# Fewer matmuls for a short contraction tile: three products of 82 rows packed into two tiles by copies within SBUF

## The chip, the cores and the metric

The kernel runs on one core of a Trainium2 chip. The metric is device time in microseconds (us) of one execution. Engines are called PE (TensorE, matmuls), ACT (ScalarE), DVE (VectorE), POOL (GpSimd) and SP (the engine that issues the DMAs).

## What is computed

A cross-attention with a gate, for 8 batches of 100 rows of width 1024 and contexts of 722 rows of width 512, in float32:

```
memory_proj = einsum('bme,de->bmd', memory, W_mem)
scores = einsum('bnd,bmd->bnm', hidden, memory_proj) / sqrt(1024)
attn = softmax(scores)
memory_context = einsum('bnm,bmd->bnd', attn, memory_proj)
gate = sigmoid(einsum('bnf,df->bnd', concat(hidden, memory_context), W_gate) + b_gate)
out = rmsnorm(hidden + gate * memory_context, norm_w)
```

The kernel multiplies by W_mem after the attention: it forms q = hidden x W_mem (width 512), scores = q x context, pc = probabilities x context (100 x 512 for a batch), and applies W_mem to pc at the end.

## The kernel before

Every float32 operand of a product is split into two fp32r tiles, a rounded `hi` (an ACT copy) and a rest `lo` = value - hi (a DVE subtraction, function `minus`, line 711). A product is then three matmuls: hi x hi, hi x lo, lo x hi.

The program is one stream of instructions for each engine, written out by hand in the order in which they run; semaphores tie the streams together. It has four stages: q for all rows; eight attention steps (`step(b, ...)`, one for each batch, in the PE, ACT and DVE streams); W_mem applied to the result (`mc_block`); the gate and the norm.

One attention step on PE:

- scores: 24 matmuls of 362 columns (line 384);
- `fill(1)`: 24 matmuls of the gate product with hidden (line 290), which need nothing of this step and lie beside the softmax;
- six transposes of the probabilities (line 398) into PSUM, once ACT's exponential is done;
- `fill(2)`: 18 more gate matmuls, beside the splitting of the transposed probabilities into `pt_hi` and `pt_lo`;
- pc: the contraction over the 722 context rows. 722 = 5 x 128 + 82, so there are MT = 5 full tiles and one of ML = 82 rows, each with three matmuls of 512 columns: 18 (line 408);
- `fill(3)`: 6 gate matmuls, while ACT scales pc;
- four transposes of pc (line 415).

The context rows (tensor `ctxN`) are loaded into `cn_stage` in three DMAs: tiles 0 to 2 (line 217), tiles 3 and 4 (line 221), and the 82 end rows (line 223). ACT rounds them into `cn_hi` (`split_ctx`, lines 542, 545 and 546) and DVE makes `cn_lo`, in two parts: part 0 (tiles 0 to 2) late in the step before, part 1 (tiles 3, 4 and the end) in the step itself. `ct_stage`, `ct_hi` and `ct_lo` are the same for the transposed context, which the scores use. All loads are issued by SP on one queue, in a fixed order: in `ahead(b)` one weight tile for the step after next (line 204), two loads of `ctxT` (line 210), then `load_ctx(b + 1)`. Each waits for the split that frees its stage buffer. In the ACT stream a step is: exponential (line 593), rounding of a weight tile (523), part 1 of the context, `pt_hi` from PSUM (600, 602), the transposed context (534), scaling pc (607), saving gate and pc (588, 612), part 0 of the next context. In the DVE stream: two maxima (780), their combination (782), the weight tile's lo part, the reciprocal of the row sums (786), `pt_lo`, part 1 of the context, the transposed context, then the saving of a gate tile (774) and q_lo.

The three matmuls of the 82-row tile are these, the last of the accumulation:

```
for lhs, rhs, part in ((pt_hi, cn_hi, 0), (pt_hi, cn_lo, 1), (pt_lo, cn_hi, 2)):
    done = nc.tensor.matmul(bank(PCB, C, N), lhs[0:rows, t, :], rhs[0:rows, t, :],
                            start=t == 0 and part == 0, stop=t == MT and part == 2)
```

Of the kernel before, what the change touches and what calls it, by code (L numbers as in the profile page):

```python
# [42 lines left out]
def build(nc, xT, ctxT, ctxN, w_mem, w_gate_x, w_mem_t, w_gate_mc, b_gate, norm_w, outT, out_rows):  # L43
# [4 lines left out]
    with top:  # L48
# [146 lines left out]
        @block.sync  # L195
        def _(sp):
            def load_x(k):
                sp.dma_start(acc[:, k, :], xT[k * P:(k + 1) * P, :]).then_inc(x_in[k], 16)

            def load_w(j, src, slot):  # L200

                if not isinstance(j, int) or j >= 2:
                    sp.wait_ge(w_lo_done, j - 1)
                sp.dma_start(w_stage[:, slot, :], src).then_inc(w_in[slot], 16)

            def load_ctxT(b, first=False):
                for s in range(2):
                    if not first:
                        sp.wait_ge(ct_lo_done, 2 * b - 1 + s)
                    sp.dma_start(ct_stage[:, 2 * s:2 * s + 2, :],  # L210
                                 ct_rows[bass.ds(b * C + s * 2 * P, 2 * P), :]
                                 .rearrange("(k p) m -> p k m", p=P)).then_inc(ct_in[s], 16)

            def load_ctx(b, first=False):
                if not first:
                    sp.wait_ge(cn_lo_done, 2 * b - 1)
                sp.dma_start(cn_stage[:, 0:3, :], cn_rows[bass.ds(b * M, 3 * P), :]
                             .rearrange("(t p) c -> p t c", p=P)).then_inc(cn_in[0], 16)
                if not first:
                    sp.wait_ge(cn_lo_done, 2 * b)  # L220
                sp.dma_start(cn_stage[:, 3:MT, :], cn_rows[bass.ds(b * M + 3 * P, (MT - 3) * P), :]
                             .rearrange("(t p) c -> p t c", p=P)).then_inc(cn_in[1], 16)
                sp.dma_start(cn_stage[0:ML, MT, :],
                             cn_rows[bass.ds(b * M + MT * P, ML), :]).then_inc(cn_in[1], 16)


            sp.dma_start(acc[:, 0, 0:H], xT[0:P, 0:H]).then_inc(x_first_in, 16)
            for i in range(2):
                cols = slice(i * C // 2, (i + 1) * C // 2)
                sp.dma_start(w_stage[:, 0, cols], w_mem[0][:, cols]).then_inc(w_first_in[i], 16)  # L230
            sp.dma_start(acc[:, 0, H:R], xT[0:P, H:R]).then_inc(x_in[0], 16)
            sp.dma_start(w_stage[:, 0, C:WB], w_mem[0][:, C:WB]).then_inc(w_in[0], 16)
            sp.dma_start(acc[:, 1, 0:H], xT[P:2 * P, 0:H]).then_inc(x_second_in, 16)
            sp.dma_start(acc[:, 1, H:R], xT[P:2 * P, H:R]).then_inc(x_in[1], 16)
            load_x(2)
            load_w(1, w_mem[1], 1)
            load_x(3)
            load_x(4)
            load_x(5)
            load_w(2, w_mem[2], 0)  # L240
            load_x(6)
            load_x(7)
            load_w(3, w_mem[3], 1)
            load_ctxT(0, first=True)
            load_ctx(0, first=True)
            sp.dma_start(bias_t[:, :], b_gate).then_inc(const_in, 16)
            sp.dma_start(norm_t[:, :], norm_w).then_inc(const_in, 16)
            load_w(J_GX, w_gate_x[0], 0)
            load_w(J_GX + 1, w_gate_x[1], 1)


            def ahead(b, slot):
                load_w(J_GX + 2 + b, wgx_rows[bass.ds((b + 2) * P, P), :], slot)
                load_ctxT(b + 1)
                load_ctx(b + 1)

            for b in range(B - 2):
                ahead(b, b % 2)
            load_w(J_MC, w_mem_t[0], 0)
            load_ctxT(B - 1)  # L260
            load_ctx(B - 1)
            load_w(J_MC + 1, w_mem_t[1], 1)
            load_w(J_MC + 2, w_mem_t[2], 0)
            load_w(J_MC + 3, w_mem_t[3], 1)
            load_w(J_G2, w_gate_mc[0], 0)


            sp.wait_ge(mc_made, 1)
            sp.dma_start(x_again[:, :, :], xT.rearrange("(k p) r -> p k r", p=P)).then_inc(xa_in, 16)
            for t in range(1, KD):  # L270
                load_w(J_G2 + t, w_gate_mc[t], t % 2)
            for k in range(0, KD, 2):
                sp.wait_ge(out_done, k + 2)
                sp.dma_start(out_v[:, k:k + 2, :], acc[:, k:k + 2, 0:FIRST]).then_inc(stored, 16)
            for i in range(ROWS2):
                sp.wait_ge(row_left, i + 1)
                sp.wait_ge(row_right, i + 1)
                sp.dma_start(out_rows[i * CHUNK:(i + 1) * CHUNK, :],
                             row_out[:, i * D:(i + 1) * D]).then_inc(stored, 16)
            sp.wait_ge(stored, 16 * (KD // 2 + ROWS2))  # L280
# [3 lines left out]
        def _(pe):  # L284
# [80 lines left out]
            def step(b, slot, cuts):  # L365
# [34 lines left out]
                fill(2)  # L400

                pe.wait_ge(pt_lo_done, b + 1)
                for t in range(MT + 1):
                    if t in (0, 3):
                        pe.wait_ge(cn_lo_done, 2 * b + 1 + t // 3)
                    rows = P if t < MT else ML
                    for lhs, rhs, part in ((pt_hi, cn_hi, 0), (pt_hi, cn_lo, 1), (pt_lo, cn_hi, 2)):
                        done = nc.tensor.matmul(bank(PCB, C, N), lhs[0:rows, t, :], rhs[0:rows, t, :],  # L408
                                                start=t == 0 and part == 0, stop=t == MT and part == 2)
                done.then_inc(pc_made, 1)  # L410
                fill(3)

                pe.wait_ge(pc_scaled, b + 1)
# [101 lines left out]
        def _(act):  # L515
# [21 lines left out]
            def split_ctx(b, part):  # L537
                if part == 0:
                    if not isinstance(b, int) or b > 0:
                        act.wait_ge(pc_made, b)  # L540
                    act.wait_ge(cn_in[0], 16 * b + 16)
                    nc.scalar.activation(cn_hi[:, 0:3, :], cn_stage[:, 0:3, :], ACT.Copy).then_inc(cn_hi_done, 1)  # L542
                else:
                    act.wait_ge(cn_in[1], 32 * b + 32)
                    nc.scalar.activation(cn_hi[:, 3:MT, :], cn_stage[:, 3:MT, :], ACT.Copy)
                    nc.scalar.activation(cn_hi[0:ML, MT, :], cn_stage[0:ML, MT, :],
                                         ACT.Copy).then_inc(cn_hi_done, 1)

            act.wait_ge(x_first_in, 16)
            nc.scalar.activation(act_hi[:, 0, 0:H], acc[:, 0, 0:H], ACT.Copy).then_inc(first_hi_done, 1)  # L550
# [158 lines left out]
        def _(dve):  # L709
# [18 lines left out]
            def split_ctx(b, part):  # L728
                dve.wait_ge(cn_hi_done, 2 * b + part + 1)
                if part == 0:  # L730
                    minus(cn_lo[:, 0:3, :], cn_stage[:, 0:3, :], cn_hi[:, 0:3, :]).then_inc(cn_lo_done, 1)
                else:
                    minus(cn_lo[:, 3:MT, :], cn_stage[:, 3:MT, :], cn_hi[:, 3:MT, :])
                    minus(cn_lo[0:ML, MT, :], cn_stage[0:ML, MT, :], cn_hi[0:ML, MT, :]).then_inc(cn_lo_done, 1)

            nc.vector.memset(idle_work[:, :], 0.0).then_inc(idle_work_set, 1)
            dve.wait_ge(first_hi_done, 1)
# [21 lines left out]
            split_w(3, 1)  # L759
            split_ctxT(0)  # L760
            split_ctx(0, 0)
            split_ctx(0, 1)
            split_w(J_GX, 0)

# [12 lines left out]
            def step(b, slot, more):  # L777
# [6 lines left out]
                split_w(J_GX + 1 + b, 1 - slot)  # L784
                dve.wait_ge(exp_done, b + 1)
                nc.vector.reciprocal(row_inv[:, :], row_sum[:, :]).then_inc(inv_set, 1)
                dve.wait_ge(pt_hi_done, b + 1)
                minus(pt_lo[:, 0:MT, :], bank(PTB, MT * N).rearrange("p (t n) -> p t n", n=N), pt_hi[:, 0:MT, :])
                minus(pt_lo[0:ML, MT, :], bank(PTB5, N, ML, KC * N), pt_hi[0:ML, MT, :]).then_inc(pt_lo_done, 1)
# [174 lines left out]
```

## Time and profile before

| | us |
|---|---|
| median of 3 runs (lowest, highest) | 299.92 (299.37, 299.94) |
| the profiled execution | 300.07 |
| its span in the profile | 298.3 |
| PE busy | 292.5 (98%) |
| DVE busy | 164.1 (55%) |
| ACT busy | 156.4 (52%) |
| mean granted PE clock | 0.996 |
| DMA packets of SP's queue, share of 16 engines' span | 45.2% |

The busy time of an engine is the time in which at least one of its instructions ran. The span is the profiled stretch from the first to the last instruction; the execution's own time has some 1.8 us around it. The DMA share of a stretch is the mean busy share of the core's 16 DMA engines. SPq and PEq stand for the engines' issuing queues, PEld for PE's weight loads, which overlap its matmuls.

### The profile page before, as it was taken

To read this page: it belongs to the slowest core of one execution; us is meant where nothing else is said; L and a number is where in the kernel's file an instruction comes from. 1 tells how busy PE (TensorE), PEld (TensorE's weight loads), DVE (VectorE), ACT (ScalarE), POOL (GpSimd) and SP (SyncE) were. 2 spreads that over 40 slices of the span, in tenths; PEclk is the share of its full clock that TensorE was granted. 3 is DMA by queue.
4 is the path that set the end of the run, shared out by engine and by line. 5 is a ranking of instruction groups with operands and counts; after the bars stand their busy time and mean duration, and the time that the engine had idled before them with its cause. 6 is when DMAs were issued, how large, how long until landed. Compare 5 with 4: busy or idle time off the path is not lost.

```text
span 298.3 us, 4078 instructions
## 1 busy us (share of the span) xinstructions
PE 292.5 (98%) x1674; PEld 281.3 (94%) x1674; DVE 164.1 (55%) x232; ACT 156.4 (52%) x227; POOL 3.0 (1%) x9
## 2 busy tenths in 40 slices
PE   8999999999999999999999999999999999999993
PEld 8999999898999989899898989999999999999993
DVE  3657454557575565855557553423457662543663
ACT  5547345454573736548363525543467773643563
POOL 0000000000000000000000000000000000010001
PEclk9999999999999999999999999999999999999998
DMA  6998391644729467383944020177223400000235
GB/s 207 406 369 268 105 357 34 229 132 135 243 99 313 149 210 247 98 265 116 288 182 145 20 70 8 64 286 294 74 70 142 141 2 1 0 2 8 109 114 211
DMA packets 18450, 46.34 MB, mean 155 GB/s; under 512 B 1520, under 2 KB 3312, under 8 KB 18432
## 3 DMA queue, kind: packets, MB, share of 16 engines
q1 hardware_dynamic: 18432, 46.09, 45.2%
q8 instruction: 13, 0.21, 0.3%
q14 instruction: 5, 0.04, 0.0%
HBM read 42.80 MB, written 3.28 MB: 154 GB/s over the span
## 4 chain that ended last, share of the span: by engine, by line
PE 98%; DVE 0%; issue 0%; DVEq 0%
PE ps L290 69%; PE ps L408 11%; PE ps L384 11%; PE ps L398 1%; PE ps L304 1%; PE ps L415 1%; PE ps L488 1%; PE ps L315 0%; PE ps L318 0%; PE ps L476 0%; DVE x_again L911 0%; PE ps L325 0%; PE ps L330 0%; PE ps L321 0%; PE ps L327 0%; PE ps L468 0%
## 5 line engine op out<-in xcount | busy, mean ns | idle before, releaser
L290 PE MATMUL ps<-act_hi,w_hi 128*128 128x400 f32 (+4 forms) x272 | 79.5, 342 | 0.0
L290 PE MATMUL ps<-act_hi,w_lo 128*128 128x400 f32 (+4 forms) x272 | 78.9, 340 | 0.0
L290 PE MATMUL ps<-act_lo,w_hi 128*128 128x400 f32 (+4 forms) x272 | 78.8, 340 | 0.0
L290 PEld LDWEIGHTS ps<-act_hi,w_hi 128*128 128x128 f32 x272 | 49.9, 188 | 0.9
L290 PEld LDWEIGHTS ps<-act_lo,w_hi 128*128 128x128 f32 x272 | 50.6, 188 | 0.1
L290 PEld LDWEIGHTS ps<-act_hi,w_lo 128*128 128x128 f32 x272 | 50.6, 188 | 0.0
L711 DVE TENSOR_TENSOR w_lo<-w_stage,w_hi 128x1024 fp32r<-128x1024 f32 (+2 forms) x23 | 26.0, 1131 | 24.3 <-ACT w_hi L523 23.2
L711 DVE TENSOR_TENSOR cn_lo<-cn_stage,cn_hi 128x1536 fp32r<-128x1536 f32 (+2 forms) x24 | 28.6, 1217 | 6.4 <-ACT cn_hi L542 5.6
L711 DVE TENSOR_TENSOR ct_lo<-ct_stage,ct_hi 128x1444 fp32r<-128x1444 f32 x16 | 25.8, 1654 | 0.5 <-ACT ct_hi L534 0.5
L523 ACT ACTIVATE w_hi<-w_stage 128x1024 fp32r<-128x1024 f32 x20 | 21.0, 1054 | 6.7 <-PE ps L290 4.9
L607 ACT ACTIVATE pc<-ps,row_inv 100x512 f32<-100x512 f32 x8 | 5.5, 687 | 34.3 <-PE ps L408 34.3
L534 ACT ACTIVATE ct_hi<-ct_stage 128x1444 fp32r<-128x1444 f32 x16 | 21.7, 1408 | 0.0
L664 ACT ACTIVATE gate<-ps,bias_t 128x384 f32<-128x384 f32 (+3 forms) x15 | 8.6, 570 | 24.6 <-PE ps L290 24.5
L384 PE MATMUL ps<-ct_hi,q_hi 128*100 128x362 f32 x64 | 21.4, 334 | 0.0
L593 ACT ACTIVATE probs<-ps,neg_top 100x722 f32<-100x722 f32 x8 | 6.9, 865 | 27.2 <-DVE neg_top L782 27.2
L384 PE MATMUL ps<-ct_hi,q_lo 128*100 128x362 f32 x64 | 21.0, 328 | 0.0
L849 DVE TENSOR_TENSOR gate<-gate,mc 128x416 f32<-128x416 f32 (+3 forms) x17 | 9.3, 550 | 21.1 <-ACT gate L664 21.1
L384 PE MATMUL ps<-ct_lo,q_hi 128*100 128x362 f32 x64 | 20.9, 327 | 0.0
L711 DVE TENSOR_TENSOR act_lo<-mc,act_hi 128x800 fp32r<-128x800 f32 x8 | 7.9, 993 | 20.5 <-ACT mc L635 20.5
L408 PE MATMUL ps<-cn_hi,pt_hi 128*100 128x512 f32 (+1 forms) x48 | 18.9, 394 | 0.0
L408 PE MATMUL ps<-cn_hi,pt_lo 128*100 128x512 f32 (+1 forms) x48 | 18.8, 392 | 0.0
L408 PE MATMUL ps<-cn_lo,pt_hi 128*100 128x512 f32 (+1 forms) x48 | 18.8, 391 | 0.0
(105 smaller groups left out, 446.2 us busy)
## 6 DMA issues: line engine op xcount, KB each, us to landing
ct_stage<-ctxT SPq DMA_DIRECT2D x16, 722.0 KB, 9.8
cn_stage<-ctxN SPq DMA_DIRECT2D x8, 768.0 KB, 5.8
cn_stage<-ctxN SPq DMA_DIRECT2D x8, 512.0 KB
w_stage<-w_gate_x SPq DMA_DIRECT2D x8, 512.0 KB, 8.9
w_stage<-w_gate_mc SPq DMA_DIRECT2D x8, 512.0 KB, 3.6
x_again<-xT SPq DMA_DIRECT2D x1, 3200.0 KB, 11.3
acc<-xT SPq DMA_DIRECT2D x6, 400.0 KB, 7.9
w_stage<-w_mem_t SPq DMA_DIRECT2D x4, 512.0 KB, 5.6
```

What stands on the lines that cost most here:

```text
L290: done = nc.tensor.matmul(o, wgt, stream[h][part], start=first and wgt is wh and part == 0, stop=last and wgt is wl, skip_group_check=onto)
L304: nc.tensor.matmul(bank(7, P), idle_work[:, :], idle_work[:, :], start=True, stop=True)
L384: done = nc.tensor.matmul(bank(h, MH + 1, N), lhs[:, k, b * N:(b + 1) * N], rhs[:, k, at:at + MH + 1], start=k == 0 and part == 0, stop=k ...
L398: done = nc.tensor.transpose(o, probs[:, t * P:t * P + rows], ident[0:N, 0:N])
L408: done = nc.tensor.matmul(bank(PCB, C, N), lhs[0:rows, t, :], rhs[0:rows, t, :], start=t == 0 and part == 0, stop=t == MT and part == 2)
L523: nc.scalar.activation(w_hi[home][:, :], w_stage[:, slot, :], ACT.Copy).then_inc(w_hi_done, 1)
L534: nc.scalar.activation(ct_hi[:, 2 * s:2 * s + 2, :], ct_stage[:, 2 * s:2 * s + 2, :], ACT.Copy).then_inc(ct_hi_done, 1)
L593: nc.scalar.activation(probs[:, :].rearrange("p (h m) -> p h m", h=2), scores, ACT.Exp, bias=neg_top[:, :], scale=float(D) ** -0.5, accum_ ...
L607: nc.scalar.activation(pc[:, :], bank(PCB, C, N), ACT.Copy, scale=row_inv[:, :]).then_inc(pc_scaled, 1)
L664: nc.scalar.activation(part, part if n < 2 else gate_bank(n), ACT.Sigmoid, bias=bias_t[:, t:t + 1]).then_inc(gate_done, 1)
L711: return nc.vector.tensor_tensor(out, whole, hi.bitcast(F32), ALU.subtract)
L849: nc.vector.tensor_tensor(part, part, mc[:, t, r0:r1], ALU.mult).then_inc(gated, 1)
```

## The change

The three products of the 82 end rows are 3 x 82 = 246 rows of contraction, and all three add into the same 100 x 512 result. They are put into two tiles, of 128 and of 118 rows:

| tile | stationary side | moving side |
|---|---|---|
| first, rows 0 to 81 | pt_hi | cn_hi |
| first, rows 82 to 127 | pt_hi, its rows 0 to 45, copied | cn_lo, its rows 0 to 45, copied |
| second, rows 0 to 81 | pt_lo | cn_hi, copied into the new tile cn_pack |
| second, rows 82 to 117 | pt_hi, its rows 46 to 81, copied | cn_lo, its rows 46 to 81, copied |

The rows change partitions, so they are copied by DMA, SBUF to SBUF, issued by SP: three copies of context rows (46, 82 and 36 rows of 2048 bytes) and two of probabilities (46 and 36 rows of 400 bytes) for each batch. PE waits for them ahead of the two packed matmuls. So that the copies can go out sooner, ACT rounds the 82 rows ahead of tiles 3 and 4, and DVE subtracts them ahead of `pt_lo` (new function `split_ctx_end`).

```diff
+SPILL = P - ML
+PACK_B = 3 * ML - P
...
+            cn_pack = sb(attn, "cn_pack", [P, C], F32R)
...
+            def pack(b):
+
+                sp.wait_ge(cn_end_lo_done, b + 1)
+                sp.dma_start(cn_hi[ML:P, MT, :].bitcast(F32), cn_lo[0:SPILL, MT, :].bitcast(F32)).then_inc(cn_packed, 16)
+                sp.dma_start(cn_pack[0:ML, :].bitcast(F32), cn_hi[0:ML, MT, :].bitcast(F32)).then_inc(cn_packed, 16)
+                sp.dma_start(cn_pack[ML:PACK_B, :].bitcast(F32), cn_lo[SPILL:ML, MT, :].bitcast(F32)).then_inc(cn_packed, 16)
+                sp.wait_ge(pt_hi_done, b + 1)
+                sp.dma_start(pt_hi[ML:P, MT, :].bitcast(F32), pt_hi[0:SPILL, MT, :].bitcast(F32)).then_inc(pt_packed, 16)
+                sp.dma_start(pt_lo[ML:PACK_B, MT, :].bitcast(F32), pt_hi[SPILL:ML, MT, :].bitcast(F32)).then_inc(pt_packed, 16)
+
             def load_ctx(b, first=False):
                 if not first:
                     sp.wait_ge(cn_lo_done, 2 * b - 1)
                 sp.dma_start(cn_stage[:, 0:3, :], cn_rows[bass.ds(b * M, 3 * P), :]
                              .rearrange("(t p) c -> p t c", p=P)).then_inc(cn_in[0], 16)
                 if not first:
+                    pack(b - 1)
                     sp.wait_ge(cn_lo_done, 2 * b)
...
             load_w(J_MC + 1, w_mem_t[1], 1)
+            pack(B - 1)
             load_w(J_MC + 2, w_mem_t[2], 0)
...
-                for t in range(MT + 1):
+                for t in range(MT):
                     if t in (0, 3):
                         pe.wait_ge(cn_lo_done, 2 * b + 1 + t // 3)
-                    rows = P if t < MT else ML
                     for lhs, rhs, part in ((pt_hi, cn_hi, 0), (pt_hi, cn_lo, 1), (pt_lo, cn_hi, 2)):
-                        done = nc.tensor.matmul(bank(PCB, C, N), lhs[0:rows, t, :], rhs[0:rows, t, :],
-                                                start=t == 0 and part == 0, stop=t == MT and part == 2)
-                done.then_inc(pc_made, 1)
+                        nc.tensor.matmul(bank(PCB, C, N), lhs[:, t, :], rhs[:, t, :],
+                                         start=t == 0 and part == 0, stop=False)
+                pe.wait_ge(cn_packed, 48 * (b + 1))
+                pe.wait_ge(pt_packed, 32 * (b + 1))
+                nc.tensor.matmul(bank(PCB, C, N), pt_hi[:, MT, :], cn_hi[:, MT, :], start=False, stop=False)
+                nc.tensor.matmul(bank(PCB, C, N), pt_lo[0:PACK_B, MT, :], cn_pack[0:PACK_B, :],
+                                 start=False, stop=True).then_inc(pc_made, 1)
...
+            def split_ctx_end(b):
+                dve.wait_ge(cn_end_hi_done, b + 1)
+                minus(cn_lo[0:ML, MT, :], cn_stage[0:ML, MT, :], cn_hi[0:ML, MT, :]).then_inc(cn_end_lo_done, 1)
```

How the instructions stand now, at three places. SP, from the last loads issued during one step to the first of the next, before:

```order
L217 DMA cn_stage<-ctxN 128x3x512 [waits cn_lo_done]
L221 DMA cn_stage<-ctxN 128x2x512 [waits cn_lo_done]
L223 DMA cn_stage<-ctxN 82x512
L204 DMA w_stage<-w_gate_x 128x1024 [waits w_lo_done]
L210 DMA ct_stage<-ctxT 128x2x722 [waits ct_lo_done] x2
```

and with the change:

```order
L233 DMA cn_stage<-ctxN 128x3x512 [waits cn_lo_done]
L223 DMA cn_hi<-cn_lo 46x512 [waits cn_end_lo_done]
L224 DMA cn_pack<-cn_hi 82x512
L225 DMA cn_pack<-cn_lo 36x512
L227 DMA pt_hi<-pt_hi 46x100 [waits pt_hi_done]
L228 DMA pt_lo<-pt_hi 36x100
L238 DMA cn_stage<-ctxN 128x2x512 [waits cn_lo_done]
L240 DMA cn_stage<-ctxN 82x512
L210 DMA w_stage<-w_gate_x 128x1024 [waits w_lo_done]
L216 DMA ct_stage<-ctxT 128x2x722 [waits ct_lo_done] x2
```

Five copies and a wait for pt_hi stand between the first and the second load of the next batch's context rows, on the same queue. DVE in the middle of a step (batches 1 to 7), before:

```order
L786 RECIPROCAL row_inv<-row_sum 100x1 [waits exp_done]
L711 TENSOR_TENSOR pt_lo<-ps,pt_hi 128x500 [waits pt_hi_done]
L711 TENSOR_TENSOR pt_lo<-ps,pt_hi 82x100
L711 TENSOR_TENSOR cn_lo<-cn_stage,cn_hi 128x1024 [waits cn_hi_done]
L711 TENSOR_TENSOR cn_lo<-cn_stage,cn_hi 82x512
```

and with the change:

```order
L811 RECIPROCAL row_inv<-row_sum 100x1 [waits exp_done]
L732 TENSOR_TENSOR cn_lo<-cn_stage,cn_hi 82x512 [waits cn_end_hi_done]
L732 TENSOR_TENSOR pt_lo<-ps,pt_hi 128x500 [waits pt_hi_done]
L732 TENSOR_TENSOR pt_lo<-ps,pt_hi 82x100
L732 TENSOR_TENSOR cn_lo<-cn_stage,cn_hi 128x1024 [waits cn_hi_done]
```

The subtraction of the 82 rows has moved ahead of the one that waits for pt_hi. PE at the end of the pc accumulation with the change (`ps` is PSUM, the second name after the arrow is the stationary side):

```order
L425 MATMUL ps<-cn_hi,pt_hi 100x512
L425 MATMUL ps<-cn_lo,pt_hi 100x512
L425 MATMUL ps<-cn_hi,pt_lo 100x512
L429 MATMUL ps<-cn_hi,pt_hi 100x512 [waits pt_packed,cn_packed]
L430 MATMUL ps<-cn_pack,pt_lo 100x512
L308 MATMUL ps<-act_hi,w_hi 128x400 x2
```

Two matmuls stand where three stood, and the first of them waits for all five copies.

## Rows read from the trace of the kernel before

**Rows 1.** Page: PE's busy time, and the engines of the chain that ended last.

```profile
PE 292.5 (98%) x1674; PEld 281.3 (94%) x1674; DVE 164.1 (55%) x232; ACT 156.4 (52%) x227; POOL 3.0 (1%) x9
...
PE 98%; DVE 0%; issue 0%; DVEq 0%
```

**Rows 2.** Waits of PE, whole span: us in total, times, longest us.

```profile
PE ps L304 <- DVE idle_work L736: 1.0, 1, 1.0
```

**Rows 3.** Chain in order of time, the pc pieces of batches 0, 2, 3: start, us.

```profile
52.48 4.13 PE ps L408 x18
...
87.86 4.13 PE ps L408 x18
...
105.55 4.13 PE ps L408 x18
```

**Rows 4.** Timeline of batch 2, sixteenth pc matmul: start us, us, engine, line.

```profile
90.91 0.16 PEld L408 LDWEIGHTS ps<-cn_hi,pt_hi 82*100 82x100 f32 x1
...
91.13 0.40 PE L408 MATMUL ps<-cn_hi,pt_hi 82*100 82x512 f32 x1
```

**Rows 5.** Timeline of ACT and DVE, and DVE's cn_lo group (ns: min/median/max).

```profile
82.80 1.05 ACT L545 ACTIVATE cn_hi<-cn_stage 128x1024 fp32r<-128x1024 f32 x1
...
84.08 0.15 DVE L786 RECIPROCAL row_inv<-row_sum 100x1 f32<-100x1 f32 x1
...
85.09 0.24 ACT L602 ACTIVATE pt_hi<-ps 82x100 fp32r<-82x100 f32 x1
...
L711 DVE TENSOR_TENSOR cn_lo<-cn_stage,cn_hi x24: 679/1211/1760, 28.5 to 175.8; 128x1536 fp32r<-128x1536 f32 x8, 128x1024 fp32r<-128x1024 f32 x8, 82x512 fp32r<-82x512 f32 x8
...
50.80 0.24 ACT L602 ACTIVATE pt_hi<-ps 82x100 fp32r<-82x100 f32 x1
```

**Rows 6.** Timeline of SP's issues around batch 2: start us, us.

```profile
79.86 0.37 SPq L217 DMA_DIRECT2D cn_stage<-ctxN  x1
87.97 0.37 SPq L221 DMA_DIRECT2D cn_stage<-ctxN  x1
88.38 0.34 SPq L223 DMA_DIRECT2D cn_stage<-ctxN  x1
```

**Rows 7.** Stretches: length, busy us by engine, PE clock, DMA share, GB/s.

```profile
84.50:85.00 0.50, 0.50 (x5) 0.50 (x5) 0.00 (x0) 0.39 (x1) 0.00 (x0) 1.00 0.10 37
...
88.50:89.00 0.50, 0.50 (x4) 0.37 (x3) 0.50 (x1) 0.00 (x0) 0.00 (x0) 1.00 0.00 0
89.00:89.50 0.50, 0.50 (x4) 0.34 (x3) 0.50 (x2) 0.00 (x0) 0.00 (x0) 1.00 0.66 98
```

**Rows 8.** Stretches in batch 6, the end of its loads.

```profile
164.00:164.40 0.40, 0.40 (x6) 0.40 (x4) 0.40 (x1) 0.09 (x1) 0.00 (x0) 1.00 0.13 51
...
166.40:166.80 0.40, 0.40 (x5) 0.39 (x4) 0.19 (x1) 0.18 (x1) 0.00 (x0) 1.00 0.10 41
166.80:167.20 0.40, 0.40 (x4) 0.40 (x3) 0.40 (x1) 0.00 (x0) 0.00 (x0) 1.00 0.00 0
```

**Rows 9.** DMA issues from 79 to 97 us: KB each, us from issue to landing.

```profile
cn_stage<-ctxN SPq DMA_DIRECT2D x1, 768.0 KB, 5.7
```

**Rows 10.** Stretches, first and last of fourteen from 89 to 103 us.

```profile
89.00:90.00 1.00, 1.00 (x7) 0.67 (x5) 1.00 (x2) 0.00 (x0) 0.00 (x0) 1.00 0.61 90
...
102.00:103.00 1.00, 1.00 (x9) 1.00 (x7) 0.00 (x0) 0.77 (x4) 0.00 (x0) 1.00 0.09 35
```

**Rows 11.** A stretch in which only stores from SBUF run.

```profile
288.50:289.00 0.50, 0.50 (x7) 0.50 (x6) 0.50 (x2) 0.41 (x1) 0.00 (x0) 1.00 1.06 409
```

**Rows 12.** Stretches at the end of the span; chain at its start.

```profile
293.00:294.00 1.00, 0.49 (x5) 0.25 (x3) 0.88 (x2) 0.81 (x2) 0.00 (x0) 1.00 0.54 221
...
296.00:297.00 1.00, 0.00 (x0) 0.00 (x0) 0.00 (x0) 0.00 (x0) 0.00 (x0) 0.58 1.02 414
...
0.99 3.81 PE ps L304 x34
4.79 0.77 PE ps L315 x2
...
6.19 0.36 PE ps L321 x2
```

More of the change, by code:

```diff
@@ L146, in build @@
         cn_hi_done, cn_lo_done = sem("cn_hi_done"), sem("cn_lo_done")
+        cn_end_hi_done, cn_end_lo_done = sem("cn_end_hi_done"), sem("cn_end_lo_done")
+        cn_packed, pt_packed = sem("cn_packed"), sem("pt_packed")
         q_hi_done, q_lo_done = sem("q_hi_done"), sem("q_lo_done")
@@ L544, in split_ctx @@
                     act.wait_ge(cn_in[1], 32 * b + 32)
-                    nc.scalar.activation(cn_hi[:, 3:MT, :], cn_stage[:, 3:MT, :], ACT.Copy)
                     nc.scalar.activation(cn_hi[0:ML, MT, :], cn_stage[0:ML, MT, :],
-                                         ACT.Copy).then_inc(cn_hi_done, 1)
+                                         ACT.Copy).then_inc(cn_end_hi_done, 1)
+                    nc.scalar.activation(cn_hi[:, 3:MT, :], cn_stage[:, 3:MT, :], ACT.Copy).then_inc(cn_hi_done, 1)
             act.wait_ge(x_first_in, 16)
@@ L732, in split_ctx @@
                 else:
-                    minus(cn_lo[:, 3:MT, :], cn_stage[:, 3:MT, :], cn_hi[:, 3:MT, :])
-                    minus(cn_lo[0:ML, MT, :], cn_stage[0:ML, MT, :], cn_hi[0:ML, MT, :]).then_inc(cn_lo_done, 1)
+                    minus(cn_lo[:, 3:MT, :], cn_stage[:, 3:MT, :], cn_hi[:, 3:MT, :]).then_inc(cn_lo_done, 1)
+            def split_ctx_end(b):
+                dve.wait_ge(cn_end_hi_done, b + 1)
+                minus(cn_lo[0:ML, MT, :], cn_stage[0:ML, MT, :], cn_hi[0:ML, MT, :]).then_inc(cn_end_lo_done, 1)
             nc.vector.memset(idle_work[:, :], 0.0).then_inc(idle_work_set, 1)
@@ L761, in _ @@
             split_ctx(0, 0)
+            split_ctx_end(0)
             split_ctx(0, 1)
@@ L786, in step @@
                 nc.vector.reciprocal(row_inv[:, :], row_sum[:, :]).then_inc(inv_set, 1)
+                if b > 0:
+                    split_ctx_end(b)
                 dve.wait_ge(pt_hi_done, b + 1)
```

## The prediction

> **What bounds the kernel now.** I read the page first. TensorE (PE) is busy 98% of the span, and the chain that ended last is PE for 98% of it [rows 1]. The list of waits then has one entry for PE, 1.0 us at the very start [rows 2]. So no load, no VectorE (DVE) and no ScalarE (ACT) step holds PE up, and a microsecond of matmuls taken away is a microsecond won, as long as nothing becomes late instead. The chain in order of time gives the price of the piece that is changed: the 18 matmuls of line 408 take 4.13 us in every batch, 0.229 us each, and two of these pieces are 105.55 - 87.86 = 17.69 us apart, which is the length of one batch step [rows 3].
>
> What could become late is the other half. Each batch now needs two tiles that five DMAs fill after the split on DVE, and PE waits for them inside line 408's accumulation. I therefore looked for three things: when the copies can start (timeline of ACT, DVE, SP), how fast a DMA with so few partitions runs (DMA share by stretches), and when PE wants the result.
>
> **The terms.** Times are those of batch b = 2 in the trace; the others repeat it.
>
> *Removed:* one matmul per batch, 8 x 0.229 = 1.84 us, all of it on the path. The two that remain have 512 columns like the rest, and 82 rows cost what 128 do, so I give them the same 0.229 us. A wait that is already fulfilled costs nothing: the wait for cn_lo before the tenth matmul leaves no gap in the 4.13 us.
>
> *When PE wants the tiles.* After 15 matmuls. Before, the sixteenth's weight load starts at 90.91 and its matmul at 91.13 [rows 4]. The new waits stand before that load, so PE stalls by (landing of the last copy - 90.91).
>
> *When the copies can start.* ACT now rounds the 82 end rows first, from 82.80 on, so they are done by about 83.4. DVE is free after the reciprocal at 84.08 + 0.15 = 84.23, and the 82x512 subtraction is the 679 ns form: done at 84.91. That fits ahead of the subtraction that waits for pt_hi, done at 85.09 + 0.24 = 85.33 [rows 5], so the move on DVE costs nothing; it uses idle time, and 0.4 us of that is left. ACT's swap costs nothing either, the same two instructions in the other order. SP waits for cn_end_lo and issues at 84.94; two issues are 0.41 us apart [rows 6], so the five go out at 84.94, 85.35, 85.76, 86.17 and 86.58, the last two after pt_hi. Data begin 1.08 us after an issue: the load of line 221 is issued at 87.97, the DMA share is 0.00 up to 89.00 and 0.66 after it [rows 6, 7]. So the first bytes of the copies flow at 86.02.
>
> *How fast they are.* This is the term that decides. The load of the 82 end rows already exists, and it is always last on its engines. With nothing behind it, the DMA share stands at 0.13 of 16 engines, which is two, and at 51 GB/s, for some 2.8 us [rows 8]. Its 82 x 2048 B at 51 GB/s are 3.3 us; a row costs an engine 80 ns. I infer that a copy is split into equal numbers of rows over at most 16 engines: 128 rows give 16, 82 give 2 (41 each). Then 46 rows give 2 (23 each) and 36 rows give 12 (3 each), and I assume that the two engines are the same ones, in order, since all copies are on one queue. The pair carries 46 + 82 + 6 = 134 rows of 2048 B, 274 KB: 5.4 us at 51 GB/s. The pair's part of the two copies of probabilities is 46 + 6 rows of 400 B. By bytes that is 0.4 us, at 80 ns a row for each engine 2.1 us; I take 0.6, since the trace's price goes with bytes. From last data to landing I take 0.6 us: a load of cn_stage is issued at 79.86 and lands 5.7 us later, at 85.6, while data flow until just before 85.0 [rows 6, 7, 9]. Sum: 86.02 + 5.4 + 0.6 + 0.6 = 92.6. PE wanted it at 90.91, a **stall of 1.7 us**. The rows for 46 and 36 partitions are my inference; the bounds are 16 engines for the 46 rows (pair: 94 rows, 3.8 us, landing 91.0, no stall) and 2 engines for the 36 rows (1.2 us more).
>
> The Trainium skill ("DMA: Bandwidth & Descriptors", on why a DMA increments its semaphore by 16) states how many engines a copy gets: the largest number up to 16 that divides its slowest dimension. The trace agrees for 82 rows (share 0.13). By that rule 46 rows also get two engines and 36 get twelve, and the sum would be the one above.
>
> *What the stall holds up.* Behind the wait on PE stand the second tile, six gate matmuls, the transposes of pc and the next scores; ACT waits for pc. Everything in a step hangs on PE's progress, so the whole step is later by the stall, and nothing later wins it back.
>
> *The queue itself.* The copies add to the two busiest DMA engines. In the period from line 221's load on, they have work from 89.0 to 102.6 (the share is 0.61 in 89 to 90 and 0.09 in 102 to 103), 13.6 us of 17.69 [rows 10]. With 5.4 + 0.6 us more they need 19.6 us a period, while PE's own step would be 17.69 - 0.23 + 1.70 = 19.16. The longer counts wherever a full set of loads stands between two packs: once the pair has no pause left, each pack starts later. The loads themselves stay in time: the end rows of the next batch would land near 97.5, and ACT wants them at 82.80 + 17.69 or later. In the last step the later issue of two weight loads (SP waits for pt_hi first) has over 10 us before their use; cost nothing.
>
> *Sum over the eight batches.* b = 0: its context copies go out early on; only the small ones wait for pt_hi (50.80 + 0.24), land near 53.5, and PE wants them at 52.48 + 3.44 = 55.9: -0.23 [rows 5, 3]. b = 1: the queue is free, -0.23 + 1.70 = +1.47. b = 2 to 6: the pair bounds, 19.6 - 17.69 = +1.9 each, 9.5. b = 7: no loads of a next batch stand in the queue (the share is 0.00 before its pack, as after 166.80 [rows 8]), +1.47. Together +12.2 us. The profiled execution took 300.07 us (span 298.3), 0.15 above the median of 299.92, so the span would be 310.5 and the time against the median **312.1 us**. Something like 0.2% (0.6 us) is what a measurement of this kernel can tell from no change.
>
> **Rivals.** (a) *The copies are hidden; faster.* It decides at 90.91: the pair's 274 KB must be through in 3.7 us, which is 74 GB/s where the row shows 51, or the 46 rows must be spread over more engines than two. Then only the matmuls count: 299.92 - 1.84 = **298.1**. For it: 82 rows alone would land in time, and the margin is only 1.7 us. Against it: the same shape on the same queue ran on two engines in each batch, and reading from SBUF is no quicker than from memory, since stores ran at 409 GB/s on 16 engines, 26 an engine [rows 11], like 51 on two. 12%.
>
> (b) *Copies within SBUF cost twice the row's price*, because reading and writing meet at the same memory. No copy of this kind is in the trace. The pair then needs 10.8 us, the landing is at 98.0 and the stall 7.1; the period by the queue is 25.0, so 5 x 7.3 + 2 x 6.9 - 0.2 = +50: **350**. Against it: loads and stores at equal price. 6%.
>
> (c) *PE's clock falls in the stalls.* At the end PE has been idle since about 293.5, and its granted clock falls to 0.58 in the stretch from 296 on. At the start, matmuls of 400 columns took 0.77 us a pair where they later take 0.36, until about 5.2 us after PE began [rows 12]. If each stall were followed by 5.2 us at half speed it would cost 2.7 us more, 7 x 2.7 = 19: **331**. Against it: the idle time in that row before the fall is over 2.5 us, longer than my stall. 5%. The Trainium skill ("TensorE: Matmul & The Clock Gate", Part 1) says that the array falls to 1.2 GHz once it has been idle and needs sustained work to return; the rows of the end and the start agree in kind.
>
> **How the numbers follow.** The forecast, a stall near 2 us in seven batches, has 77%. Its own bounds: with the pair 10% quicker and no bound by the queue the stall is 1.1 us, +6, 306; with the start another 0.4 us earlier, 303. Upward: the 36 rows on two engines +8, the small rows at 80 ns each +10, one of them 320 to 322, some of both 325. The range 303 to 325 leaves out (a), (b), (c) and little of the forecast. Faster: (a) less the case where it just misses, 0.11; within 0.2%: 0.03; slower: 0.86.
>
> **What would show it.** In the profile after: a new wait of PE on the copies (line 429 on DMA of cn_pack, cn_hi or pt_lo), seven times, 1.5 to 2.5 us each, none in b = 0; the matmuls before it at 0.229 us; period 19 to 20 us; in the copies' stretch a DMA share of 0.13 near 51 GB/s, beginning about 1.1 us after the first issue, and no pause of the pair between steps 2 and 6; PE's clock still 1.00. The prediction is wrong if the share in that stretch is well over 0.2 (then (a)), if it stays at 0.13 with half the GB/s (then (b)), or if no wait appears on PE at all.

## The result and the profile after

The changed kernel takes 342.59 us (median of 6 runs, 341.52 to 343.84) against 299.80 us before: 14.3% slower, ratio 1.1431 with a 95% interval of 1.1402 to 1.1461. The profiled span is 339.9 us. The direction and the cause of the wait were as predicted, the size was not: +12.2 us were forecast, +42.8 came, and the range ended at 325.

The page of the changed kernel: busy times, the granted clock in 40 slices, the engines of the chain that ended last.

```profile
PE 302.8 (89%) x1666; PEld 288.7 (85%) x1666; DVE 164.1 (48%) x232; ACT 156.5 (46%) x227; POOL 3.0 (1%) x9
...
PEclk9999999997998989979979979979999999999999
...
PE 57%; DMA 16%; DVE 10%; ACT 6%; SPq 6%; issue 3%; DVEq 0%
```

PE has 8 matmuls fewer than in [rows 1], and is busy longer: some of them run at a lower clock. The chain was PE for 98%; now 16% of it is DMA. PE's waits, of which before there was only one, at the start:

```profile
PE ps L429 <- DMA pt_lo<-pt_hi: 31.3, 7, 5.0
PE ps L322 <- DVE idle_work L760: 1.0, 1, 1.0
```

Seven waits on the packed copies, 4.5 us each to the matmul's start (the first batch has none). The chain still shows the 15 matmuls of the first batch at their old price, 0.229 us each, so PE is no slower while the clock is up (start, us):

```profile
52.46 3.44 PE ps L425 x15
```

Now one of the stalls. SP's issues in batch 2:

```profile
90.52 0.63 SPq L223 DMA_DIRECT2D cn_hi<-cn_lo  x1
91.19 0.61 SPq L224 DMA_DIRECT2D cn_pack<-cn_hi  x1
91.85 0.76 SPq L225 DMA_DIRECT2D cn_pack<-cn_lo  x1
92.65 1.03 SPq L227 DMA_DIRECT2D pt_hi<-pt_hi  x1
93.72 0.74 SPq L228 DMA_DIRECT2D pt_lo<-pt_hi  x1
...
114.31 0.63 SPq L223 DMA_DIRECT2D cn_hi<-cn_lo  x1
```

The period is 114.31 - 90.52 = 23.8 us where it was 17.69 [rows 3]. PE around the wait (in brackets the idle time before the matmul, and what ended it), then the chain's piece for the last copy, from the start of its issue to its landing:

```profile
96.58 0.39 PE L425 MATMUL ps<-cn_hi,pt_lo 128*100 128x512 f32 x1
101.51 0.70 PE L429 MATMUL ps<-cn_hi,pt_hi 128*100 128x512 f32 x1 [4.54 <-DMA pt_lo<-pt_hi]
102.01 0.63 PE L430 MATMUL ps<-cn_pack,pt_lo 118*100 118x512 f32 x1
```

```profile
93.72 7.65 DMA pt_lo<-pt_hi
```

The copies have landed at 101.37, 10.85 us after the first issue. On the way the two DMA engines were slow for a while: their share is 0.12 or more, but only 18 to 29 GB/s flow, where [rows 8] has 51 (columns as in [rows 7]):

```profile
94.00:94.50 0.50, 0.50 (x3) 0.33 (x2) 0.50 (x1) 0.00 (x0) 0.00 (x0) 1.00 0.16 29
94.50:95.00 0.50, 0.50 (x4) 0.34 (x3) 0.50 (x2) 0.00 (x0) 0.00 (x0) 1.00 0.19 29
95.00:95.50 0.50, 0.50 (x4) 0.37 (x3) 0.50 (x1) 0.00 (x0) 0.00 (x0) 1.00 0.12 18
```

I call this the dip. The stretches around the end of the wait:

```profile
98.00:99.00 1.00, 0.00 (x0) 0.00 (x0) 0.00 (x0) 0.00 (x0) 0.00 (x0) 1.00 0.88 166
...
102.00:103.00 1.00, 1.00 (x4) 0.89 (x3) 0.00 (x0) 0.32 (x1) 0.00 (x0) 0.50 1.02 348
103.00:104.00 1.00, 1.00 (x4) 0.99 (x4) 0.00 (x0) 0.37 (x1) 0.00 (x0) 0.50 1.06 290
...
105.00:106.00 1.00, 1.00 (x8) 0.99 (x7) 0.25 (x1) 0.77 (x2) 0.00 (x0) 1.00 0.12 45
```

PE is idle from 96.97 on, and from about 101.5 to 105 its granted clock is 0.50, the lower of its two levels (1.2 instead of 2.4 GHz): a packed matmul takes 0.70 us instead of 0.40. So each of the seven batches pays a stall and then a slow stretch. Of the prediction's signs, the wait came as told, seven times and none in the first batch; its length (1.5 to 2.5 us), the period (19 to 20 us) and the clock (1.00) did not.

### The profile page after: what moved, and what is told of

Same layout as the page of the kernel before. It is cut to its first block, busy times and chain, and to the rows that moved or that the text cites. A ratio compares the mean times of both kernels' runs of the same rounds, so it can differ in the third digit from the quotient of the medians.

```text
span 339.9 us, 4110 instructions
## 1 busy us (share of the span) xinstructions
PE 302.8 (89%) x1666; PEld 288.7 (85%) x1666; DVE 164.1 (48%) x232; ACT 156.5 (46%) x227; POOL 3.0 (1%) x9
## 4 chain that ended last, share of the span: by engine, by line
PE 57%; DMA 16%; DVE 10%; ACT 6%; SPq 6%; issue 3%; DVEq 0%
PE ps L308 47%; DMA pt_lo<-pt_hi 16%; DVE cn_lo L732 5%; ACT cn_hi L563 3%; DVE w_lo L732 3%; SPq L227 2%; ACT w_hi L544 2%; DVE top_score L805 2%; SPq L225 2%; PE ps L429 1%; SPq L223 1%; PE ps L436 1%; SPq L224 1%; PE ps L402 1%; PE ps L322 1%
## 5 line engine op out<-in xcount | busy, mean ns | idle before, releaser
L308 PE MATMUL ps<-act_hi,w_hi 128*128 128x400 f32 (+4 forms) x272 | 81.5, 350 | 0.0
L308 PE MATMUL ps<-act_hi,w_lo 128*128 128x400 f32 (+4 forms) x272 | 81.3, 350 | 0.0
L308 PE MATMUL ps<-act_lo,w_hi 128*128 128x400 f32 (+4 forms) x272 | 81.1, 349 | 0.0
L308 PEld LDWEIGHTS ps<-act_hi,w_hi 128*128 128x128 f32 x272 | 51.6, 194 | 1.7
L308 PEld LDWEIGHTS ps<-act_hi,w_lo 128*128 128x128 f32 x272 | 52.6, 195 | 0.1
L308 PEld LDWEIGHTS ps<-act_lo,w_hi 128*128 128x128 f32 x272 | 52.3, 194 | 0.1
L429 PE MATMUL ps<-cn_hi,pt_hi 128*100 128x512 f32 x8 | 4.9, 608 | 31.3 <-DMA pt_lo<-pt_hi 31.3
L429 PEld LDWEIGHTS ps<-cn_hi,pt_hi 128*100 128x100 f32 x8 | 1.6, 198 | 34.3 <-DMA cn_pack<-cn_lo 34.3
L799 DVE COPY acc<-ps 128x400 f32<-128x400 f32 x8 | 4.6, 574 | 53.1 <-PE ps L308 53.1
L732 DVE TENSOR_TENSOR q_lo<-ps,q_hi 128x400 fp32r<-128x400 f32 x16 | 9.0, 575 | 20.4 <-ACT q_hi L633 17.4
## 6 DMA issues: line engine op xcount, KB each, us to landing
ct_stage<-ctxT SPq DMA_DIRECT2D x16, 722.0 KB, 12.2
```

Of the source, the lines that this page charges most:

```text
L308: done = nc.tensor.matmul(o, wgt, stream[h][part], start=first and wgt is wh and part == 0, stop=last and wgt is wl, skip_group_check=onto)
L429: nc.tensor.matmul(bank(PCB, C, N), pt_hi[:, MT, :], cn_hi[:, MT, :], start=False, stop=False)
L732: return nc.vector.tensor_tensor(out, whole, hi.bitcast(F32), ALU.subtract)
```

## The experiments

Theory A: the stall is set by how many rows stand on the two DMA engines (the pair) to which copies of 46 and 82 rows are confined. Rivals: the number of issues and their fixed time (B), the queue itself (C), a price of reading from SBUF (D), and later what a pause on that pair belongs to (E, F, G).

### Fewer rows on the pair

**even_counts**, 42 and 40 rows in the tiles instead of 46 and 36:

```diff
-SPILL = P - ML
-PACK_B = 3 * ML - P
+SPILL = 42
+PACK_A, PACK_B = ML + SPILL, 2 * ML - SPILL
```

> The end rows are divided 42 and 40 between the tiles instead of 46 and 36; the 82-row copy stays. The pair of DMA engines then has 41 + 3 + 4 = 48 rows of 2048 B a batch instead of 67, and no small rows to speak of (3 + 4 instead of 26). Theory A (the rows on the pair of engines set the landing): 19 rows of 80 to 110 ns and the small rows go, 2.0 to 2.9 us less a stall, so a stall of 2 to 3 us where the changed kernel has 4.5 to 5, and 320 to 329 us. Rival B (the issue time on SP, 0.6 to 1.0 us a copy, and a fixed time of landing set it): as the changed kernel, 340 to 344 us.

319.4 us, ratio 1.0652 (1.0611 to 1.0693), at the quick end of A and far from B. The wait of PE is 2.5 us instead of 4.5, and the mean granted clock is 0.980 to 0.995 in the four executions, where the changed kernel has 0.931 to 0.965:

```profile
PE ps L429 <- DMA pt_lo<-pt_hi: 17.3, 7, 2.9
```

**act_fills**, ACT in place of the 82-row DMA:

```diff
-                sp.dma_start(cn_pack[0:ML, :].bitcast(F32), cn_hi[0:ML, MT, :].bitcast(F32)).then_inc(cn_packed, 16)
...
+                act.wait_ge(cn_end_hi_done, b + 1)
+                nc.scalar.activation(cn_pack[0:ML, :], cn_hi[0:ML, MT, :].bitcast(F32), ACT.Copy).then_inc(cn_pack_set, 1)
```

> The 82-row copy of cn_hi into cn_pack is made by ACT (one more 82x512 activation after pt_hi) and its DMA goes; 46 and 36 rows stay. The pair has 26 rows instead of 67. Theory A: 41 rows of 80 to 110 ns go, 3.3 to 4.5 us, the stall falls to 0.3 to 1.5 us and PE's clock stays at 1.00: 300 to 310 us. Rival B: only one issue of some 0.65 us goes, 334 to 339 us.

298.42 us, ratio 0.9947 (0.9931 to 0.9964): a little better than A's range, because no stall is left at all, and faster than before the change. B is out.

**even_and_act**, both edits:

> Both edits: the 42/40 division and ACT in place of the 82-row copy. No engine has more than 7 rows of context a batch. Theory A: no stall is left, the saved matmul shows, 298 to 299 us. Rival B: four issues, the last near 2.9 us after the first, and a landing some 2 us behind, 5 us after the first issue where PE comes after 6: also no stall, or one below 1 us, 298 to 305 us. If a stall of over 2 us stays, both are wrong.

298.36 us, ratio 0.9944 (0.9927 to 0.9961), as A said.

**eighty_and_two** is the sharpest of these. All bytes are still moved by DMA, with one issue more; only the row count of one copy is different:

```diff
-                sp.dma_start(cn_pack[0:ML, :].bitcast(F32), cn_hi[0:ML, MT, :].bitcast(F32)).then_inc(cn_packed, 16)
+                sp.dma_start(cn_pack[0:80, :].bitcast(F32), cn_hi[0:80, MT, :].bitcast(F32)).then_inc(cn_packed, 16)
+                sp.dma_start(cn_pack[80:ML, :].bitcast(F32), cn_hi[80:ML, MT, :].bitcast(F32)).then_inc(cn_packed, 16)
```

> The changed kernel, all its bytes copied by DMA as before, but the 82-row copy is issued as one of 80 rows and one of 2. If the rows are shared out in equal numbers, 80 rows run on 16 engines, 5 each, and the pair has 23 + 5 + 1 + 3 = 32 rows instead of 67. Theory A: 35 rows go, 3 to 4 us, against one more issue of 0.65 us: a stall of 0 to 2 us, 298.5 to 312 us. Rival B (number of issues and bytes): 342 to 348 us.

297.93 us against 299.78, ratio 0.9936 (0.9914 to 0.9958): 44.7 us below the changed kernel. PE waits only at the start, and two pc pieces in the chain are 17.46 us apart, one matmul less than 17.69:

```profile
87.24 3.44 PE ps L426 x15
90.67 0.23 PE ps L430
90.91 0.23 PE ps L431
...
104.70 3.44 PE ps L426 x15
```

This version, like the two with ACT, is quicker than both kernels. Measured again, with five executions:

> The kernel of eighty_and_two, with five rounds beside the kernel before: theory A: 297.7 to 298.5 us, the ratio's interval below 1.00. Rival B: 299 us or more.

298.05 us, ratio 0.9941 (0.9928 to 0.9953). And with 42 and 40 rows as well:

> 42 and 40 rows, and the 82-row copy as 80 + 2: no copy but the 2-row one is confined to two engines. Theory A: no stall, PE bound, 1.84 us below the kernel before: 297.7 to 298.5 us. Rival B (six issues of 0.65 us bound it): 299 us or more.

298.09 us, ratio 0.9949 (0.9936 to 0.9961), the same: once the copies are in time, spreading them further gives nothing.

### The queue without the wait

**copies_aside**: the five copies go to the same rows, but PE does the three matmuls of 82 rows and waits for none of them.

```diff
+                    if t == MT:
+                        pe.wait_ge(cn_end_lo_done, b + 1)
...
+                    if b > 0:
+                        act.wait_ge(cn_packed, 48 * b)
```

> The five copies are issued as in the changed kernel, but PE does the three matmuls of 82 rows as before and does not wait for them; who overwrites their sources waits for them a step later. Theory A, with the wait as the only cost: 299.5 to 301 us, as before the change. Rival C (the queue itself or the copies' traffic in SBUF slows the other engines or makes the loads late): over 303 us, with waits of ACT on loads of cn_stage or w_stage.

307.56 us, ratio 1.0264 (1.0241 to 1.0288): A's expectation here is wrong and C is right. The copies cost time although nobody in the step reads them. SP's issues of two first copies, ACT's new wait, and the chain's piece for the load it waits for:

```profile
84.70 0.63 SPq L223 DMA_DIRECT2D cn_hi<-cn_lo  x1
...
104.32 0.63 SPq L223 DMA_DIRECT2D cn_hi<-cn_lo  x1
```

```profile
ACT cn_hi L569 <- DMA cn_stage<-ctxN: 16.8, 7, 3.8
```

```profile
89.27 13.64 DMA cn_stage<-ctxN
```

This period is 19.62 us. The five from 84.70 on are 18.2 to 20.0 us, 19.4 on average, against the prediction's bound by the pair's work, 19.6. The bound appears as ACT waiting for the load of the 82 end rows, which stands behind the copies on the same two engines; in the stretches between 84 and 104.5 the DMA share is nowhere below 0.12, so the pair has no pause.

### The clock

**keep_busy**: matmuls whose result nobody reads fill the stall.

```diff
+                    for _ in range(72):
+                        nc.tensor.matmul(bank(7, P), idle_work[:, :], idle_work[:, :], start=True, stop=True,
+                                         skip_group_check=True)
```

> The changed kernel with 72 matmuls of 128 bf16 columns (into an unused bank, nothing reads them) ahead of the wait for the copies in batches 1 to 7, some 4 us in which PE stood idle. They fit into the stall of 4.5 us. Theory A with a clock part (the stall is 4.5 to 5 us a batch, and the fall of the granted clock after it costs 1.5 us more): the clock stays at 1.00, the period falls from 23.8 to about 22.3 us, 330 to 334 us. Rival (the clock costs nothing, since the path goes over something else): 341 to 345 us.

330.87 us, ratio 1.1031 (1.1008 to 1.1055), within A with a clock part. The mean granted clock is 1.000 where the changed kernel has 0.965:

```profile
core 0: 329.3 us, clock 1.000
```

```profile
91.97 7.75 DMA pt_lo<-pt_hi
```

The copies land as late as before (7.75 us after the last issue, 7.65 in the changed kernel), and in six of the seven batches PE still waits for them behind the added matmuls, 0.3 to 0.9 us, so these did not outlast the stall there (in the last batch they just fill it). The whole difference, 342.59 - 330.87 = 11.7 us or 1.7 us a batch, is the clock. That is half of the 3.4 us or so of the slow stretch.

### What makes the landing late

**from_memory**: the three context copies keep their shapes, but read from memory and write rows that nobody reads; PE does the three matmuls of 82 rows. One of the three copies:

```diff
-                sp.dma_start(cn_pack[0:ML, :].bitcast(F32), cn_hi[0:ML, MT, :].bitcast(F32)).then_inc(cn_packed, 16)
+                sp.dma_start(cn_pack[0:ML, :], cn_rows[bass.ds(b * M, ML), :]).then_inc(cn_packed, 16)
```

> The three context copies keep their shapes and sizes, but read rows of the context from memory instead of cn_lo and cn_hi, into rows that nothing reads; PE does the three matmuls of 82 rows and waits for all five copies, so the result of the copies is not part of the computation. Theory A (rows on the pair, whatever their source): as the changed kernel plus one matmul a batch, 341 to 347 us. Rival D (a row read from SBUF costs more than one read from memory; the pauses of the pair come from that): the pair needs 5.4 us for its rows instead of 7.6, the stall is some 2 to 2.5 us, 318 to 330 us.

334.14 us, ratio 1.1147 (1.1096 to 1.1197), between the two: 8.5 us quicker than the changed kernel, although it has one matmul more a batch (1.84 us in all). Its issues are shorter, and the wait is 2.9 us instead of 4.5:

```profile
90.54 0.26 SPq L223 DMA_DIRECT2D cn_stage<-ctxN  x1
90.84 0.30 SPq L224 DMA_DIRECT2D cn_pack<-ctxN  x1
91.18 0.33 SPq L225 DMA_DIRECT2D cn_pack<-ctxN  x1
```

```profile
PE ps L430 <- DMA cn_pack<-ctxN: 20.2, 7, 3.9
```

The same shapes read from SBUF took 0.61 to 0.76 us to issue. The dip is shorter: none shows in batch 2 (41 and 53 GB/s from 92.5 to 93.5), and in batch 3 it lasts one microsecond at 29 and 37 GB/s. So the source matters in part, yet a stall well above the forecast 1.7 us stays.

**no_small_copies**: the copies of probabilities are issued in the first batch only.

```diff
+                if b == 0:
```

> The two copies of probabilities are left out from batch 1 on (PE reads stale rows there, so that part of the product is not computed). Theory A: 0.9 us of small rows on the pair go, and the landing is that of the context copies, 1 to 1.5 us sooner: 331 to 336 us, or down to 326 if the clock stays up. Rival B (the issue of the last copies and their own landing set it): the stall would all but go, below 315 us.

339.27 us, ratio 1.1318. Neither range holds it. The wait is shorter, as A said (3.5 us instead of 4.5), which is worth 7 us, but only 3.3 us came. In the profiled executions the mean clock is 0.945 instead of 0.965. Over all executions, though, the changed kernel has 0.931 to 0.965 and this one 0.939 to 0.949, so the clock does not account for the rest, and where it went stays open:

```profile
PE ps L431 <- DMA cn_pack<-cn_lo: 24.4, 7, 4.1
```

**loads_after**: SP holds the next loads back until the copies have landed.

```diff
                     pack(b - 1)
+                    sp.wait_ge(cn_packed, 48 * b)
+                    sp.wait_ge(pt_packed, 32 * b)
```

> The changed kernel with SP waiting until the five copies have landed before it issues the next loads (end of cn_stage, weights, ctxT), which then start some 5 us later and still have 8 us before their use. In the changed kernel the pair of DMA engines pauses for about 2 us in the middle of its rows, when SP issues these loads. Theory E (issuing and running the loads behind the copies starves the pair): no pause, the pair needs 5.5 us instead of 7.6, the stall is 2 to 3 us: 317 to 330 us. Rival F (the pause belongs to the copies themselves): 340 to 346 us.

334.07 us, ratio 1.1168 (1.1134 to 1.1201), between E and F. The chain's piece from the last issue to the landing starts at 92.84 and lasts 6.68 us; the first issue was at 89.47:

```profile
89.47 0.63 SPq L223 DMA_DIRECT2D cn_hi<-cn_lo  x1
```

```profile
92.84 6.68 DMA pt_lo<-pt_hi
```

That is 10.05 us from first issue to landing instead of 10.85 (batch 2 of each). The loads behind the copies are worth 0.8 us of it, not 2.

**small_after**: SP also holds back the copies of probabilities, so nothing follows the context copies.

```diff
+                sp.wait_ge(cn_packed, 48 * (b + 1))
                 sp.wait_ge(pt_hi_done, b + 1)
```

> As loads_after, and SP also waits until the three context copies have landed before it issues the two copies of probabilities, so that nothing is issued behind the context copies while they run. The copies of probabilities then land some 3 us after that, so the whole time says little (335 to 345 us); the question is how long the context copies take. Theory G (any DMA issued behind makes the pair pause): the DMA share stays at 0.13 with about 50 GB/s from first to last row, and the small copies are issued 7.5 to 8 us after the first context copy. Rival F (the pause belongs to the copies): a dip in GB/s of about 2 us again, 9 to 10 us.

350.0 us (ratio 1.1655), not 335 to 345, but the question was the pair. Stretches of half a microsecond, with only the context copies under way (first issue at 91.60):

```profile
95.50:96.00 0.50, 0.50 (x4) 0.36 (x3) 0.50 (x2) 0.00 (x0) 0.00 (x0) 1.00 0.19 29
96.00:96.50 0.50, 0.50 (x4) 0.36 (x3) 0.50 (x1) 0.00 (x0) 0.00 (x0) 1.00 0.11 25
96.50:97.00 0.50, 0.50 (x4) 0.36 (x3) 0.50 (x1) 0.00 (x0) 0.00 (x0) 1.00 0.06 20
97.00:97.50 0.50, 0.50 (x4) 0.37 (x3) 0.37 (x1) 0.00 (x0) 0.00 (x0) 1.00 0.13 29
97.50:98.00 0.50, 0.50 (x4) 0.19 (x2) 0.00 (x0) 0.00 (x0) 0.00 (x0) 1.00 0.13 33
...
98.50:99.00 0.50, 0.00 (x0) 0.00 (x0) 0.00 (x0) 0.00 (x0) 0.00 (x0) 1.00 0.13 49
```

The pair runs at 49 GB/s from 98.5 to 100, close to the 51 of [rows 8], but at 20 to 33 GB/s from 95.5 to 98.0. The stretches from 93.0 to 100.5 add up to some 332 KB, and the three copies have 336 KB, so the pair needed about 7.3 us (to 100.3) for rows priced at 5.4. The dip is there with nothing behind the copies, and SP could issue the small copies only 9.2 us after the first one (at 100.80). F holds, G falls.

**only_82**: from batch 1 on only the 82-row copy, with the loads held back.

```diff
+                if b == 0:
+                    sp.dma_start(cn_hi[ML:P, MT, :].bitcast(F32), cn_lo[0:SPILL, MT, :].bitcast(F32)).then_inc(cn_packed, 16)
```

> From batch 1 on only the 82-row copy is issued, the other four are left out (those rows are stale, so that part of the product is not computed), and the next loads wait for it. 41 rows on each engine of the pair. Theory A by 84 ns a row: 3.4 us of data, landing 5.1 to 5.5 us after the issue, PE comes 6 us after it: no stall, 298 to 300 us. Rival F (a pause of 2 us inside this copy): landing near 7.5 us, a stall of 1 to 2 us, 305 to 313 us.

304.09 us, ratio 1.0126 (1.0097 to 1.0155), just below F's range, but in most batches not for F's reason. In batch 2 there is no dip:

```profile
86.50:87.00 0.50, 0.50 (x4) 0.47 (x3) 0.50 (x1) 0.50 (x1) 0.00 (x0) 1.00 0.13 49
87.50:88.00 0.50, 0.50 (x4) 0.34 (x3) 0.50 (x2) 0.00 (x0) 0.00 (x0) 1.00 0.13 49
88.50:89.00 0.50, 0.50 (x4) 0.36 (x3) 0.50 (x1) 0.00 (x0) 0.00 (x0) 1.00 0.13 49
...
90.00:90.50 0.50, 0.47 (x3) 0.01 (x1) 0.00 (x0) 0.00 (x0) 0.00 (x0) 1.00 0.13 49
90.50:91.00 0.50, 0.00 (x0) 0.00 (x0) 0.00 (x0) 0.00 (x0) 0.00 (x0) 1.00 0.01 4
```

The copy was issued at 83.97, and the pair was still at work on the held-back loads then; it ends at 90.5, when PE has just run out of matmuls. In batches 3 to 6 it is the same. Here the late loads make the copy late, and the rival comes near the time with the wrong mechanism.

Batch 1 is different. Its copy was issued at 66.52, the earlier rows ran out near 67.0 (share 0.07 and 0.04 in the next two stretches), and the single copy has the dip:

```profile
69.00:69.50 0.50, 0.50 (x4) 0.48 (x4) 0.50 (x1) 0.50 (x1) 0.00 (x0) 1.00 0.16 29
69.50:70.00 0.50, 0.50 (x4) 0.34 (x3) 0.50 (x1) 0.10 (x1) 0.00 (x0) 1.00 0.11 29
...
70.50:71.00 0.50, 0.50 (x4) 0.37 (x3) 0.50 (x2) 0.00 (x0) 0.00 (x0) 1.00 0.14 53
```

The five copies of copies_aside show the same two cases in one kernel. Issued at 104.32, while the pair was at work, it moves at 46 GB/s or more up to 109, where other transfers hide it. Issued at 181.58, on engines with nothing to do (share 0.00), the copies have the dip:

```profile
108.00:108.50 0.50, 0.50 (x4) 0.36 (x3) 0.50 (x1) 0.50 (x1) 0.00 (x0) 1.00 0.14 53
...
185.50:186.00 0.50, 0.50 (x4) 0.37 (x3) 0.00 (x0) 0.00 (x0) 0.00 (x0) 1.00 0.19 33
```

**big_first**: the 82-row copy issued ahead of the 46-row one.

> The changed kernel with the 82-row copy issued ahead of the 46-row one. Theory A: the pair has the same rows, 340 to 345 us. If the pause stands at a boundary between two copies or after a number of rows, its place in time tells: after 41 rows (a boundary) about 5 us after the issue, or at the same 3.5 us as in the changed kernel.

342.04 us (ratio 1.139), in A's range, but partly by luck: PE's wait is 3.6 us a batch instead of 4.5, and the mean granted clock is 0.926 and 0.936 in the two executions, in place of 0.931 to 0.965.

```profile
PE ps L429 <- DMA pt_lo<-pt_hi: 24.9, 7, 4.0
```

The stretches do not tell where the pause stands, since the rows of the pair are mixed with those of the 36-row copy and of the loads; this one is inconclusive on that.

## Why the prediction was wrong in size

Point by point, by the prediction's own steps:

- *Removed.* Right. 15 matmuls take 3.44 us, the two packed ones 0.23 us each at full clock (eighty_and_two), the period without a stall is 17.46 us.
- *When the copies can start.* Right: the first issue in the changed kernel is at 90.52, 6.1 us before the sixteenth weight load could start; forecast 84.94 and 90.91, 6.0 us. The moves on ACT and DVE cost nothing. The first batch has no stall.
- *How many engines.* Right, and it is the cause: 82 rows cut into 80 and 2, and nothing else, take the whole loss away.
- *The price of a row.* Right outside the dip: 49 GB/s within SBUF (small_after), where the load from memory had 51 [rows 8]. Rival (b), a doubled price, falls, although the total lies not far from its 350 us.
- *The landing.* **This is the step that failed.** The forecast was 92.6 - 84.94 = 7.7 us from first issue to landing; measured are 10.85. "The pair carries ... 5.4 us at 51 GB/s" left out the dip, in which the pair moves at 18 to 33 GB/s; with it the same rows took about 7.3 us (small_after), 1.9 more. I had taken the price from the last part of a load, when its engines had long been at work. The loads behind the copies add 0.8 us (loads_after), and the copies of probabilities are worth 1.0 us of PE's wait (no_small_copies) where I gave them 0.6. These come from three runs and together make 3.1 of the 3.15 us, so this split is an estimate. The five issues also took 3.2 us where I spread them over 1.6; no run shows what that alone costs. The stall is thus 4.7 us (330.87 - 299.80 + 1.84, over seven batches) where the forecast was 1.7: +21 us.
- *The clock.* Rival (c) came true on top of the forecast. I had set it aside because the idle time before the fall [rows 12] was longer than my stall of 1.7 us; with a stall of over 4 us that reason was gone, and the two risks should have been tied together. Waits of 2.5 us in even_counts left the clock at 0.980 or more, so for a stall of 1.7 us the reason may well have held. +11.7 us, or 1.7 us a stall where the rival had 2.7. The Trainium skill ("TensorE: Matmul & The Clock Gate", Part 1) has a fall to 1.2 GHz after idleness; the granted clock of 0.50 behind each stall agrees.
- *The queue bound.* Near as a number (19.4 us on average in copies_aside, forecast 19.6), but it did not bind here, because the stalls stretched the period past it: 0.4 us a batch in five batches less.

The sum: 12.2 - 2.2 (queue bound not reached) + 21 + 11.7 = 42.7 us, measured 42.8. It closes by construction, since both the 4.7 us and the 11.7 us are taken from keep_busy's time. What checks the stall apart from that is PE's own wait in the changed kernel, 4.5 us a batch.

The prediction names the Trainium skill ("DMA: Bandwidth & Descriptors", on why a DMA increments its semaphore by 16) for the number of engines. What eighty_and_two and even_counts show agrees: 80 rows divide by 16, 42 by 14, 40 by 10, while 82 and 46 have no divisor between 2 and 16 but 2 itself, and both edits shorten the wait.

Rival (a), a hidden copy and 298.1 us, is what the kernel gives once the row count is changed: 298.05.

What stays open: why the pair has the dip. It needs neither loads nor small copies behind (small_after) nor several copies in a row (batch 1 of only_82). The traces tie it to how soon the pair comes to the copies; the times are estimates from bytes and GB/s. In batches 2 to 6 of only_82 it came to the copy some 3 to 4 us after the issue (168 KB at 49 GB/s, counted back from the end), and there is no dip. In the changed kernel, in batch 1 of only_82, in small_after and in loads_after it came to the first copy after some 1 to 1.8 us, and there is one, in the last two even though it was at work until then. No run varied this alone, and why it should matter is not shown. The wait in from_memory, 1.6 us a batch shorter, says that the source or its longer issue has a part.

## What to carry to other kernels

Before a DMA goes onto the path, look at its row count: 82 or 46 rows ran on two engines of sixteen, and cutting 82 into 80 + 2 was worth 44.7 us here. A transfer confined to few engines also queues ahead of later loads on those engines, so it can cost time with nobody waiting for it. And when a forecast contains a stall of PE, price the clock's fall with it: the two are one risk, and the fall added over a third to what the stall cost.

## What the runs showed of the hardware that I had not expected

- An SP issue of a context copy with an SBUF source took 0.61 to 0.76 us, the same shapes from memory 0.26 to 0.33 us.
- Two DMA engines that came to a copy within SBUF 1 to 1.4 us after its issue moved at 18 to 37 GB/s for 1.5 to 2.5 us (the changed kernel, small_after, batch 1 of only_82), then at 49 GB/s or more; where they came to it 3 us or more after the issue (only_82, batches 2 to 6), they kept 49 GB/s.
- Shorter waits did not raise the clock: with 3.5 or 3.6 us a batch (no_small_copies, big_first) the mean granted clock was 0.926 to 0.949, with 4.5 us (the changed kernel) 0.931 to 0.965, and only with 2.5 us (even_counts) 0.980 or more.
- Time at the lower clock did not cost in proportion: executions of the changed kernel with a mean clock of 0.965 took 341.5 and 341.7 us, those with 0.931 took 342.8 and 343.5 us, while filling the stalls gave back 11.7 us.
